# Layer 0 opens from x in SBUF: group norm inside the layer, image 1's on ScalarE, first convolutions by halves

## What is computed

```python
def _gn(v, G=32, eps=1e-5):
    g = v.reshape(B_, G, C_ // G, H_, W_)
    m = mean(g, axis=(2, 3, 4)); s = var(g, axis=(2, 3, 4))
    return ((g - m) / sqrt(s + eps)).reshape(v.shape)

def _L0_conv_ref(x, ...):                       # x is _gn(x)
    qkv = einsum('bchw,oc->bohw', x, w_qkv) + b_qkv
    qkv = depthwise_conv_3x3(qkv, w_dw) + b_dw
    q, k, v = split(qkv)                        # 4 heads of 48 channels, 4096 pixels
    q = q / norm(q, axis=channels); k = k / norm(k, axis=channels)
    attn = softmax(einsum('bhdn,bhdm->bhnm', q, k) * temperature)
    out = einsum('bhnm,bhdm->bhdn', attn, v)
    return einsum('bchw,oc->bohw', out, w_proj) + b_proj

x = x + _L0_conv_ref(_gn(x), ...)
x = x + _L1_conv_ref(_gn(x), ...)
```

## Time and profile before

| | us |
|---|---|
| median of 3 runs | 3560.64 |
| the profiled execution | 3561.09 |
| its span, first to last instruction | 3559.3 |
| outside the span | 1.8 |
| last z store landed, layer 0's first DMA issued | 65.75 |
| first score matmul of head 0 | 236.39 |
| PE busy in the span | 3188.6 (90%) |
| VectorE busy | 1988.1 (56%) |
| ScalarE busy | 2096.1 (59%) |
| GpSimd busy | 1019.1 (29%) |

### The profile page before, as it was taken

The page is one execution under the profiler, slowest core; times in us unless marked ns, Lnnn a source line. Parts: engine busy times, 40 slices in busy tenths (PEclk is TensorE's granted clock), DMA queues, the critical chain, the costliest instruction groups (busy, mean ns, idle before and its releaser), DMA issues. The chain is left out here.

```text
span 3559.3 us, 48038 instructions
## 1 busy us (share of the span) xinstructions
PE 3188.6 (90%) x16424; PEld 1279.7 (36%) x16424; DVE 1988.1 (56%) x2522; ACT 2096.1 (59%) x2306; POOL 1019.1 (29%) x510
## 2 busy tenths in 40 slices
PE   1239999999999999999999966899999858999998
PEld 0012232222322323223222222455555424555555
DVE  4655243752257432563420145688888555888886
ACT  0015655556556565564666612688888415888886
POOL 1210202102021020020200003366566432666565
PEclk9669999999999999999999988999999979999999
DMA  6131212212103111131110033477777724877777
GB/s 179 45 77 28 60 42 45 57 45 55 50 24 77 44 37 50 35 78 32 25 44 7 10 90 92 102 139 146 145 143 139 159 75 99 145 138 144 145 144 132
DMA packets 691175, 295.71 MB, mean 83 GB/s; under 512 B 603314, under 2 KB 645042, under 8 KB 689266
## 3 DMA queue, kind: packets, MB, share of 16 engines
q1 hardware_dynamic: 690996, 293.45, 38.7%
HBM read 95.46 MB, written 34.28 MB: 36 GB/s over the span
## 5 line engine op out<-in xcount | busy, mean ns | idle before, releaser
L440 ACT ACTIVATE prob<-ps_s,cur 128x1024 f32<-128x1024 f32 x1024 | 1084.5, 1110 | 738.4 <-PE ps_s L514 736.8
L527 PE MATMUL ps_a<-prob,vt 128*64 128x512 f32 x4096 | 997.2, 608 | 0.0
L1132 POOL TENSOR_TENSOR p_lo<-gp,p_hi 128x1024 f16<-128x1024 f32 x256 | 551.9, 2166 | 402.9 <-ACT p_hi L1231 397.8
L1359 PE MATMUL ps_s<-kst,qs 128*128 128x512 f16 x2560 | 639.2, 383 | 20.3 <-DMA qs<-q_scratch 12.1
L1372 PE MATMUL ps_o<-v_hl,at_hi 128*128 128x384 f16 x2048 | 546.8, 328 | 28.4 <-DMA at_lo<-p_lo 26.9
L508 PE MATMUL ps_s<-q_a,k_a 128*128 128x512 f16 x2048 | 535.1, 383 | 7.6 <-issue 2.6
L1372 PE MATMUL ps_o<-v_hl,at_lo 128*128 128x192 f16 x2048 | 504.6, 247 | 0.0
L1606 DVE TENSOR_SCALAR_CACHE_REDUCE neg<-ps_s,mix 128x1024 f32<-128x1024 f32 x256 | 327.2, 1278 | 131.7 <-PE ps_s L1359 130.4
L527 PEld LDWEIGHTS ps_a<-prob,vt 128*64 128x64 f32 x4096 | 249.4, 136 | 412.4 <-issue 410.3
L1359 PEld LDWEIGHTS ps_s<-kst,qs 128*128 128x128 f16 x2560 | 244.8, 99 | 247.0 <-issue 23.3
L508 PEld LDWEIGHTS ps_s<-q_a,k_a 128*128 128x128 f16 x2048 | 138.0, 97 | 517.1 <-ACT prob L440 437.2
(11 more groups left out here) (176 smaller groups left out, 2763.2 us busy)
## 6 DMA issues: line engine op xcount, KB each, us to landing
z<-z_scratch SPq DMA_DIRECT2D x96, 384.0 KB, 3.9
sq<-rn_scratch SPq DMA_DIRECT2D x16, 768.0 KB, 10.6
qs<-q_scratch SPq DMA_DIRECT2D x64, 128.0 KB, 2.8
gn_x<-in_x SPq DMA_DIRECT2D x4, 1536.0 KB, 18.7
z_scratch<-gn_x SPq DMA_DIRECT2D x4, 1536.0 KB, 11.6
q_a<-hi SPq DMA_DIRECT2D x64, 96.0 KB, 2.4
rden<-den_scratch SPq DMA_DIRECT2D x64, 96.0 KB, 2.2
o_scratch<-o_s SPq DMA_DIRECT2D x64, 96.0 KB, 1.9
```

The costliest lines, as they stand in the source:

```text
L440: act.activation(prob[:, a % PR, :], ps_s[:, a % 2, :], ACT.Exp, bias=cur[:, slot:slot + 1], scale=1.0 / SPLIT).then_inc(exped, 1)
L527: ins = pe.matmul(ps_a[h * HALF:(h + 1) * HALF, j % 2, :], vt[:, slot, m, :], prob[:, a % PR, h * CH:(h + 1) * CH], start=(m == 0), stop=( ...
L1132: pool.tensor_tensor(p_lo[:, cols], prob[s][:, cols], p_hi[:, cols], ALU.subtract).then_inc(lo_made[c], 1)
L1359: ins = pe.matmul(ps_s[:, c % 2, h * CH:(h + 1) * CH], qs[:, s, qt, :], kst[:, ktile, cols], start=(t == 0), stop=(t == len(terms) - 1))
```

## The change

- The separate group norm block is gone. `layer0` allocates `xin` itself, in the memory that q_a, k_a, q_b, k_b and part of `prob` take later, and loads image 0 in half tiles.
- Image 0: VectorE takes the statistics of its two tiles. VectorE normalises the first tile, ScalarE the second, in halves. PE projects the first two tiles (q, k and v) straight from `xin` (`project_first`), not from z. z is stored to DRAM for the later tiles only.
- Image 1: sums, squares and the normalising run on ScalarE (passes over 4096 columns with a running sum), the power and its refinement on GpSimd.
- ScalarE moves the first two tiles into `pad`, squares q and k, moves the sums, and makes `hi`; VectorE makes `lo`. The norms of head 0 come from ScalarE's Sqrt and VectorE's reciprocal.
- `conv_half` runs nine taps of one half, then of the other; each tap waits for the one before it. ScalarE may refill the upper rows of `pad` when the first half of q and k is done.
- Broadcast of the norms of head 0 in four pieces (`rn_first`), and z of tile 2 is loaded behind `split_out`.
- In every head, `split` has one `tensor_tensor` of 112 rows for `u` where it had two of 48.

```diff
@@ layer0, SP @@
+                for h in range(2):
+                    for t in range(CT):
+                        cols = slice(h * N // 2, (h + 1) * N // 2)
+                        sp.dma_start(xin[:, t, cols], x[0, t * CP:(t + 1) * CP, cols]).then_inc(x_in[t][h], 16)
...
-                load_z(range(4), 0, 0, None)
-                load_z(range(4, 8), 0, 0, 1)
-                load_z(range(4), 1, 0, 5)
-                sums_out(10, 0)
-                load_z(range(4, 8), 1, 0, 11)
-                norms_out(0)
-                load_z(range(4), 2, 0, 15)
+                for t in range(CT):
+                    sp.dma_start(xin[:, CT + t, :], x[1, t * CP:(t + 1) * CP, :]).then_inc(x_in[CT + t][0], 16)
...
+                sums_first(0)
+                for t in range(CT):
+                    sp.wait_ge(z1_made, t + 1)
+                    sp.dma_start(z_dram[1, t * CP:(t + 1) * CP, :], xin[:, CT + t, :]).then_inc(z_out, 16)
+                sums_first(1)
+                sp.wait_ge(ss_out, 64)
...
+                for c in range(4):
+                    cols = slice(c * NB, (c + 1) * NB)
+                    for h in range(2):
+                        sp.dma_start(sq[h * HALF:h * HALF + HD, cols],
+                                     rn_dram[h:h + 1, cols].partition_broadcast(HD)).then_inc(rn_first[c], 16)
+                sp.wait_ge(z_out, 16 * 2 * CT + 16 * CT)
+                sp.wait_ge(help_full, 18)
                 split_out(0, 0, None)
+                load_z(range(4), 2, 0, None)
@@ layer0, PE @@
+                def project_first(slot, c, use):
+                    n, bank = use
+                    helper_free(n)
+                    pe.wait_ge(z_low, 1 + c // 4)
+                    pe.wait_ge(z_high, 1 + c // 4)
+                    for t in range(CT):
+                        ins = pe.matmul(ps_h[0:KR, bank, :], w[:, slot, t, 0:KR], xin[:, t, c * CH:(c + 1) * CH],
+                                        start=(t == 0), stop=(t == CT - 1))
+                    ins.then_inc(help_full, 1)
@@ layer0, VectorE, split of every head @@
-                        for h in range(2):
-                            r = slice(h * HALF, h * HALF + HD)
-                            ins = dve.tensor_tensor(u[r, :], qk[r, cols], sq[r, cols], ALU.mult)
-                        ins.then_inc(unit_op, 1)
+                        dve.tensor_tensor(u[:, :], qk[:, cols], sq[:, cols], ALU.mult).then_inc(unit_op, 1)
@@ layer0, VectorE, the opening @@
+                def conv_half(slot, dst, tiles, h, n_free, taps=range(TAPS)):
+
+                    dve.wait_ge(help_free, n_free)
+                    for tap in taps:
...
+                            dve.wait_ge(conv_op, CONV_OPS * tiles + TAPS * h + tap)
...
+                conv_half(0, qk, 0, 0, 5)
+                conv_half(0, qk, 0, 1, 8)
+                conv_half(1, vv, 1, 0, 14, range(5))
                 norms_ask(0)
+                conv_half(1, vv, 1, 0, 14, range(5, 6))
+                dve.wait_ge(powed, 1)
+                dve.reciprocal(nry[:, :, :], nry[:, :, :]).then_inc(rooted_n, 1)
...
                 norms(0)
+                conv_half(1, vv, 1, 0, 14, range(6, TAPS))
+                unit(0)
+                conv_half(1, vv, 1, 1, 18, range(1))
+                for c in range(4):
+                    low(c)
+                    if c < 3:
+                        unit(c + 1)
+                    conv_half(1, vv, 1, 1, 18, range(1 + 2 * c, 3 + 2 * c))
```

More of the change, by code:

```diff
@@ L189, in layer0 @@
         lo = sb("lo", [KR, 2, NB], F16)
+        NT = B * CT
+        with ExitStack() as start:
+            xin = sb("gn_x", [CP, NT, N], F32, start)
         q_a = sb("q_a", [P, 2, N], F16)
@@ L245, in layer0 @@
         rooted = sem("rooted")
+        x_in = [[sem(f"x_in{i}_{h}") for h in range(2)] for i in range(NT)]
+        group_in = sem("group_in")
+        gn_op = sem("gn_op")
+        gn_asked = sem("gn_asked")
+        gn_full = sem("gn_full")
+        gn_pow_asked = sem("gn_pow_asked")
+        gn_powed = sem("gn_powed")
+        z_low = sem("z_low")
+        z_high = sem("z_high")
+        gn1_op = sem("gn1_op")
+        gn1_pow = sem("gn1_pow")
+        z1_made = sem("z1_made")
+        z_out = sem("z_out")
+        rn_first = [sem(f"rn_first{c}") for c in range(4)]
+        rooted_n = sem("rooted_n")
         STEPS = NBL * KT
@@ new lines, in _ @@
+                act.wait_ge(gn_full, 4)
+                act.wait_ge(gn_powed, 1)
+                act.activation(var1[:, :], ps_a[0:CP, 1, 8:8 + CT], ACT.Identity, bias=tiny[:, 0:1],
+                               scale=1.0 / N).then_inc(gn1_op, 1)
+                square(0)
+                square(1)
+                evac_sums(0)
+                act.wait_ge(w_in[1], 48)
+                for c in range(3):
+                    evac_project(1, c, 9)
+                act.wait_ge(gn1_pow, 5)
+                for t in range(CT):
+                    act.activation(shift1[:, t:t + 1], away1[:, t:t + 1], ACT.Copy, scale=gy1[:, t:t + 1]).then_inc(gn1_op, 1)
@@ new lines, in _ @@
+                act.wait_ge(gn1_op, 8)
+                for t in range(CT):
+                    act.activation(xin[:, CT + t, :], xin[:, CT + t, :], ACT.Identity,
+                                   bias=shift1[:, t:t + 1], scale=gy1[:, t:t + 1]).then_inc(z1_made, 1)
+                evac_project(1, 3, CONV_OPS)
+                square(2)
+                evac_project(1, 4, CONV_OPS)
+                square(3)
+                evac_sums(1)
+                for c in range(5, 8):
+                    evac_project(1, c, CONV_OPS)
```

294 lines of the change are left out of this document (175 added, 119 removed).

## The result

The kernel after takes 3457.72 us, the median of 4 runs (3455.09 to 3459.09); the kernel before took 3559.76 on the same chips (4 runs, 3556.55 to 3561.38). The ratio is 0.9714, with a 95% interval from 0.970 to 0.973. Forecast were 3453.0 us and a range from 3442 to 3469. The profiled execution of after took 3457.56 us with a span of 3455.7 and a mean granted clock of 0.965.

A forecast was written before the change was run, and what follows sets the result against it. The opening's single chain to the first score and PE, with three waits for v's last tap in the heads, were taken as bounds. 3561.1 - 92.4 (opening) - 16.0 (heads) = 3452.7 us; likeliest 3453, range 3442 to 3469.

The forecast's parts named there:

- Opening: From the start to the first score: at 144 us instead of 236.4, 92.4 us gained.
- the price of a dependent tap: VectorE's convolution in the opening: each tap waits for the one before, some 2.37 us instead of 2.27.
- GpSimd's five small steps: Image 1's group norm in the opening: they run under the three chunks of v and add no time.
- v's chunks: Three chunks of v in the opening, PE starting at 64.4: 8.7 us, so done at 73.1.
- Heads: One `u` instead of two frees PE's three waits for v's last tap and the slow stretches behind: 16.0 us gained.
- 9.4 us after the last tap: First `evac_vt` copy in odd heads keeps this distance, so done at 684.7; 0.3 us of PE wait may remain, once.
- A: Opening later by 5 to 15 us through near-level steps priced from other shapes; taken 3460 us; chance 0.22.
- B: Head waits stay: `u` at 112 rows no faster, or VectorE loses the gain before the last tap; 3469 us; chance 0.08.
- C: Opening shorter by 4 to 10 us: taps as cheap as before, broadcast at 3.3, splits sooner; 3445 us; chance 0.13.
- SP's 35 us: End of the opening: SP issues four pieces of split_out at 8.75 us each without a pause, bounding the split.
- D: Slower than before: ScalarE's six passes over 4096 columns run far longer than priced; 3565 us; chance 0.01.
- E: Opening not shortened because z_out, which split_out waits for, lands late, by 107 us; folded into A.

The follow-up runs named there:

- pad40: The kernel after with 40 idle one-column copies at the start of ScalarE's program; 3452.28 us, one run.
- u_pair: The kernel after with the one `u` of 112 rows put back into two of 48 in the heads after the first; 3474.85 us.
- u_one: The kernel before with only the one `u` of 112 rows in place of two of 48; 3539.77 us, ratio 0.9934.
- late_z1: The kernel after with ScalarE's second normalising pass of image 1 and its store moved behind v's chunks and the squares; 3457.85 us.
- act_issue: The kernel after with ScalarE's queue issuing the 8 DMAs of each `hi` in the opening, SP only the 6 of each `lo`; 3445.95 us.
- old52: The kernel before with 52 idle one-column copies ahead of head 0 on ScalarE; 3562.58 us, one run.

## Why the prediction was right, and where it was not

**Opening, 92.4 forecast, 91.8 measured.** Step by step, forecast and measured: normalising from 24.6 and 23.1; PE from 26.5 and 25.4; eight chunks in `pad` at 43.9 and 43.4; tap to tap 2.37 and 2.39 ((19.06 - 2.35) / 7), which bears out the price of a dependent tap; q and k done at 79.4 and 79.2; summing passes with their reading 3.7 and 3.7 to 3.8; v's first half from 83.0 and 82.89, with a wait of 3.6 and 3.74; broadcast issued at 99.8 and 99.59; `u` at 105.3 and 104.92; pieces of SP 8.75 and 8.86, 8.86 and 9.23 us apart; first score at 144 and 144.57. The Trainium skill ("VectorE: DVE Perf Modes", The DRAIN you can't avoid) says that a semaphore after each operation costs nothing. By that a tap would have taken 2.27 us, and the rows speak against it with 2.39. The Trainium skill ("ScalarE: Activation LUTs", What ACT_TABLE_LOAD costs) puts a change of table at about 2.66 us. That was not met either: the load took 1.28 us and the Sqrt came right behind, 1.30 in all.

Two of these were right with a wrong step inside. GpSimd's five small steps, which I put at nothing under the chunks of v, took 9.6 us (60.09 to 69.66, up to 2.31 each against 0.69 for the first). The last three start at 62.57, 64.96 and 67.35, 2.39 us apart like VectorE's taps beside them. The chunks ended at 72.8, so 3.1 us of cover were left. And v's chunks are not as fixed as I had them. PE starts that projection after standing, and the table by stretch shows this of after:

```profile
64.00:68.00 4.00, 4.00 (x5) 1.61 (x6) 3.93 (x3) 0.83 (x2) 3.83 (x3) 0.50 0.01 4
68.00:72.00 4.00, 4.00 (x9) 1.53 (x8) 3.95 (x2) 1.14 (x2) 1.65 (x1) 0.80 0.00 0
```

PEclk is 0.50, the 1.2 GHz level, and then 0.80. In pad40 the same two stretches read 0.53 and 1.00, and ScalarE's normalising started at 72.07 against 73.26. Over the eleven kernels whose code is the same up to there, but for idle copies, it started from 70.51 to 73.47. In the seven of them that share the whole opening the first score came from 142.80 to 144.76. So one execution each of the same opening code differs by 2 us and more, and the forecast's agreement to 0.6 us is partly luck.

**Heads, 16.0 forecast, 10.2 measured.** The mechanism held: no wait for vv, clock 1.00, the first two transposes 3.6 us apart. u_pair and u_one show it to be the cause. Two terms were mis-sized. The sentence that the first `evac_vt` comes "9.4 us after the last tap" and leaves 0.3 us took a distance for a chain: the copy stands behind block 2's reciprocal, which waits for a DMA, and not behind the tap. Counted alike, it came 10.25 us after the last tap (583.62 to 593.87) and left 1.25 us in head 1, of 1.95 in all three heads. That is 1.6 us together with the smaller stalls. The larger term, 3.45 us, had no line in the sum at all. I took it that the heads' ScalarE code, being unchanged, would cost the same; it had been moved by 52 instructions, and its back branch cost 3.3 and 3.0 us instead of 2.6 and 2.7, with nothing to cover the difference. The remaining 0.7 us is spread.

**Rivals.** A (a later opening) didn't occur, but late_z1 shows its store in the way of nrm to be real. B (head waits stay) is refuted by after, and u_pair gives its price in the heads: 17.0 us, of which 1.6 are a dearer border. C (a shorter opening) didn't occur. Taps cost 2.39, and SP's 35 us stayed, as the reservation in C said; act_issue shows VectorE's chain 3.9 us behind SP's queue. D and E didn't occur: ScalarE's passes were within 0.2 us of their price, and the stores of z had landed long before split_out.

## What to carry to other kernels

Sum an opening engine by engine, and price the queue that issues the DMAs like an engine: here it was the last bound, and giving 8 of its 14 issues to an idle queue was worth 3.9 us. Compare two kernels from the last point up to which their code is the same, and not from the start of the span: here the openings stood up to 2 us apart before an edit could act. When an edit adds or removes instructions on an engine that runs a loop later, look at that loop's back branch in both traces before explaining a difference of a few us; a handful of idle instructions at a place that waits anyway is a cheap test. A wait that follows another within a few us can be hidden by it, or by the slow clock behind it, so the gain of removing the first is its length less what the second then shows.

## What the runs showed of the hardware

- ScalarE's loop back branch takes 2.4 to 2.7 us to the next instruction (20 borders), and 3.0 to 3.3 where two 8 KB packets of instructions follow it within 0.5 us of each other (8 borders). A second queue, q8, carries instruction packets of 16 KB; that these are PE's is inferred, no run showed it.
- Four small steps of GpSimd (96x2) beside VectorE's taps took 1.62 to 2.31 us each, where the step ahead of them took 0.69.
- A load of 32 KB issued 0.37 us behind a store of 1.5 MB on the same queue landed after 7.0 us; the seven others of its kind in that run took 1.7 to 1.9 (late_z1).
- 14 small DMA issues took SP 8.75 us without a pause; giving 8 of them to ScalarE's queue took 3.9 us off the time from `u` to the first score (act_issue).
- A stall of PE of 2.66 us left the following matmuls at full clock in one execution (old52), one of 2.85 did not in another.
